# Category-conditioned matmul and ternary FFN on one core: the second product of two steps back issued ahead of the transposes of one step back

## The reference

```python
selected_W = W[cat_ids]
selected_b = b[cat_ids]
out = jnp.einsum('bsd,bdh->bsh', x, selected_W) + selected_b[:, None, :]
...
w_scale = jnp.mean(jnp.abs(weight)) + EPS
u = weight / w_scale
w_quant = u + jax.lax.stop_gradient(jnp.clip(jnp.round(u), -1.0, 1.0) - u)
a_scale = jnp.max(jnp.abs(x), axis=-1, keepdims=True) + EPS
z = jnp.clip(x / a_scale * 127.0, -128.0, 127.0)
a_quant = z + jax.lax.stop_gradient(jnp.round(z) - z)
y = jnp.einsum('bsi,oi->bso', a_quant, w_quant)
y = y * (w_scale * a_scale / 127.0)
...
x = x + _L0_ffn_ref(_L0_cond_ref(x, itok_B_0_63, L0_cond_W, L0_cond_b), L0_ffn_weight)
```

## Time and profile before

| | before |
|---|---|
| median of 3 runs | 546.17 us (544.36 to 547.55) |
| the profiled execution's own time | 543.38 us |
| its span, first to last instruction | 541.5 us |
| TensorE busy with matmuls | 512.7 us, 95% |
| VectorE, ScalarE, GpSimd busy | 392.5, 343.7, 281.2 us |
| TensorE clock granted, mean | 0.998 of 2.4 GHz |
| HBM traffic | 172.6 MB, 319 GB/s over the span |

### The profile page before, as it was taken

One profiled execution on the slowest core, in us unless ns is written; L12 is line 12 of the kernel. 1 busy time (PEld: TensorE's weight loads), 2 busy tenths in 40 slices (PEclk: granted clock), 3 DMA queues, 4 the chain that ended last, 5 costly groups with the idle time before them and its releaser, 6 DMA issues.

```text
span 541.5 us, 13855 instructions
## 1 busy us (share of the span) xinstructions
PE 512.7 (95%) x2584; PEld 355.8 (66%) x2585; DVE 392.5 (72%) x652; ACT 343.7 (63%) x502; POOL 281.2 (52%) x396
## 2 busy tenths in 40 slices
PE   4799999999999999999999998999989999999996
PEld 1576667666776666677676665667657677777774
DVE  3787765879667968966866858776797868758763
ACT  3577565765676567666756666766766666666753
POOL 3695455444556364555554463555446455565540
PEclk9999999999999999999999999999999999999999
DMA  5899879998899999979989889987999999899963
GB/s 170 276 404 351 291 258 310 382 364 274 324 364 343 367 333 392 356 243 372 350 291 294 325 322 398 365 288 271 407 332 363 329 363 342 273 310 333 323 194 117
DMA packets 71728, 172.76 MB, mean 319 GB/s; under 512 B 8096, under 2 KB 8224, under 8 KB 64800
## 3 DMA queue, kind: packets, MB, share of 16 engines
q1 hardware_dynamic: 71712, 172.59, 90.0%
HBM read 139.00 MB, written 33.55 MB: 319 GB/s over the span
## 4 chain that ended last, share of the span: by engine, by line
PE 35%; DVE 6%; issue 5%; DVEq 2%; ACT 2%; DMA 2%; ACTq 0%; SPq 0%; POOL 0%; POOLq 0%
PE ps_cond L619 9%; PE ps_cond L621 8%; PE ps_cond L620 8%; PE ps_y L587 8%; DVE sb_w_lo L486 3%; PE ps_aT L597 2%; DVE sb_absmax L527 2%; DMA sb_bias<-cond_b 2%; DVEq L165 1%; ACT sb_a_rounded L406 1%; ACT sb_w_hi L355 1%; DVE sb_a_step L530 0%; ACTq L165 0%; DVE sb_x_rows L520 0%; DVEq L486 0%
## 5 line engine op out<-in xcount | busy, mean ns | idle before, releaser
L619 PE MATMUL ps_cond<-sb_w_hi,sb_xT_hi 128*128 x512 | 220.7, 431 | 6.7 <-issue 3.2
L621 PE MATMUL ps_cond<-sb_w_hi,sb_xT_lo 128*128 x512 | 200.3, 391 | 0.0
L620 PE MATMUL ps_cond<-sb_w_lo,sb_xT_hi 128*128 x512 | 199.4, 389 | 0.0
L486 DVE TENSOR_TENSOR sb_w_lo<-sb_w_raw,sb_w_hi x106 | 162.1, 1567 | 20.2 <-issue 16.8
L317 POOL TENSOR_TENSOR sb_xT_lo<-sb_xT_raw,sb_xT_hi 128x512 fp32r<-128x512 f32 x128 | 166.4, 1300 | 10.9
L527 DVE TENSOR_REDUCE sb_absmax<-ps_cond 128x1 f32<-128x512 f32 x128 | 87.7, 686 | 100.6 <-PE ps_cond L621 89.1
L406 ACT ACTIVATE sb_a_rounded<-ps_cond,sb_rounder,sb_a_inv 128x512 f32<-128x512 f32 x128 | 99.5, 777 | 94.9 <-DVE sb_a_inv L533 94.5
L334 POOL TENSOR_SCALAR sb_y_scale<-sb_absmax,sb_w_step 128x1 f32<-128x1 f32 x128 | 41.0, 320 | 224.6 <-DVE sb_absmax L527 224.3
L587 PE MATMUL ps_y<-sb_ffnT,sb_aT 128*128 128x512 bf16 x512 | 131.2, 379 | 1.6 <-DVE sb_ffnT L512 0.9
L619 PEld LDWEIGHTS ps_cond<-sb_w_hi,sb_xT_hi 128*128 128x128 f32 x512 | 96.2, 188 | 51.7 <-issue 27.2
L396 ACT ACTIVATE sb_aT<-ps_aT 128x512 bf16<-128x512 int16 x128 | 75.4, 589 | 67.5 <-PE ps_aT L597 62.8
(11 more groups left out here) (69 smaller groups left out, 36.2 us busy)
## 6 DMA issues: line engine op xcount, KB each, us to landing
sb_w_raw<-cond_w SPq DMA_DIRECT2D x53, 1024.0 KB, 6.6
sb_xT_raw<-x_t SPq DMA_DIRECT2D x128, 256.0 KB, 5.1
sb_x_rows<-x SPq DMA_DIRECT2D x128, 256.0 KB, 5.2
out<-sb_x_rows SPq DMA_DIRECT2D x128, 256.0 KB, 4.9
sb_bias<-cond_b SPq DMA_DIRECT2D x54, 256.0 KB, 7.9
sb_ffn_raw<-ffn_t SPq DMA_DIRECT2D x1, 1024.0 KB, 6.9
sb_w_raw<-cond_w SPq DMA_DIRECT2D x4, 256.0 KB, 6.7
sb_cat_row_i<-itok SPq DMA_DIRECT2D x1, 64.0 KB, 3.5
```

Source lines behind the costliest of these rows:

```text
L486: dve.tensor_tensor(w_lo[:, bass.ds(at, PIECE)], w_raw[:, bass.ds(at, PIECE)], w_hi[:, bass.ds(at, PIECE)].bitcast(F32), ALU.subtract).the ...
L619: pe.matmul(ps_cond, x_hi_k, w_hi_k, start=False, stop=False, skip_group_check=True)
L620: pe.matmul(ps_cond, x_hi_k, w_lo_k, start=False, stop=False, skip_group_check=True)
L621: last_mm = pe.matmul(ps_cond, x_lo_k, w_hi_k, start=False, stop=(k == KD - 1), skip_group_check=True)
```

## The change

In TensorE's `body` the call of `second_product` for step r-2 now stands ahead of the call of `a_transpose` for step r-1. Nothing else is edited: the same instructions with the same waits are issued, in another order. The last step's extra calls stay where they are.

```diff
                 last_mm.then_inc(cond_mm_done, 1)
+                if not first or u >= Y_BEHIND:
+                    second_product(r - Y_BEHIND, (u - Y_BEHIND) % U, first)
                 if not first or u >= 1:
                     a_transpose(r - 1, (u - 1) % U, first)
-                if not first or u >= Y_BEHIND:
-                    second_product(r - Y_BEHIND, (u - Y_BEHIND) % U, first)
                 if last and u == U - 1:
```

## The result

The changed kernel takes 548.9 us as the median of 14 runs (547.26 to 551.08); the kernel before, run beside it, 546.15 us (14 runs, 543.98 to 547.79). The ratio is 1.0054, 95% interval 1.0036 to 1.0073. So the change costs 2.75 us, where 1.1 us less was forecast. The time lies at the upper end of the range of 541.5 to 549.5, just over the 2.7 us beyond which a slower kernel had been given 14%.

The account below looks back on a forecast made before the run. TensorE was taken to bound the kernel, losing 26.1 us in few late steps. Terms -2.3 + 0.4 + 0.24 + 0.6 = -1.1 us put the median at 546.2 - 1.1 = 545.1 us, range 541.5 to 549.5.

Parts of the forecast that it names:

- the later of C + 1.1 and A + chain: Start of TensorE's next step in a late step; 1.1 us is transposes plus second product, chain the sequencer's work behind A.
- C: Time in a step when TensorE is free, its last first-product matmul being done; 127.55 in step 27 before.
- A: Time when a_rounded, the rounding that the transposes wait for, ends; 128.60 in step 27 before.
- The gain in late groups, -2.3: Late steps joined where VectorE never waited: 19 groups, 17 saving 0.13 us each at the chain's front, plus 0.1.
- the bounds set (12 and 25): Sign of error: more than 25 or fewer than 12 late groups would mean VectorE's lag was changed by something left out.
- Slow reads, +0.4: The longest table read, 2149 ns in an on-time step, would start 0.4 us later; bounds 0 and 0.8.
- The end, +0.6: At the program's end the transposes of step 127 follow the second product of step 126, delaying all behind by 0.6 us.
- The start, +0.24: Transposes formerly done while the first second product waited for the ternary weight now follow it: 0.24 us more.
- ScalarE later by up to 0.5, hidden with 1 us to spare: Later transposes delay ScalarE's PSUM move, so a_rounded comes up to 0.5 us later in on-time steps, at no cost.
- rival 3: ScalarE becomes the late one: the later move delays rounding 0.5 us in late groups; +8.2 us, 554.4; chance 10%.
- Rival 1: The sequencer runs past the transposes' wait, so late groups lose up to 1.1 us less; -14.0, 532.2 us; chance 8%.
- Rival 2: Nothing saved at the front of the chain in late steps, only costs remain: +1.2, 547.4 us; chance 22%.

Follow-up runs that it names:

- the split order: Three of the second product's four matmuls ahead of the transposes, the fourth behind them, against the kernel before: 545.25 us, ratio 0.9969.
- the narrow last piece in the old order: Kernel before, no transposes moved, last second-product matmul of each step cut into 384 and 128 columns, narrow piece last: 548.59 us, ratio 1.0031.
- The two kernels without the split: Old and changed order, VectorE's split of the weights' low part left out from the second group of steps on: 523.5 and 529.34 us.
- both kernels with the bias three ahead: Three-plus-one second-product order and changed order, table read before the transposes' wait, bias written three steps ahead instead of two: 536.41 and 542.0 us.
- the split order with the early read and the bias two ahead: Three second-product matmuls, transposes, fourth matmul, with the next step's table read before the transposes' wait, against the kernel before: 540.69 us, ratio 0.9899.

## Why the prediction was wrong

- **The step that failed** is the sentence on the later of C + 1.1 and A + chain, "the first is the same sum in either order". It is not. In the old order the last thing ahead of the next first product is a matmul of 0.216 us, under which a float32 weight load disappears; in the new one it is a transpose of 0.056 us, and 0.055 us of the load shows. That is 6.5 us in 119 steps, and with the 19 ns inside the first product 8.7. TensorE's own part of the steps that are on time was costed at nothing, without comparing what stands at their end. Both numbers were there in the trace of before, a load of 0.19 us and transposes four to 0.24 us. Two experiments show the cause from either side: the split order (3.847 again) and the narrow last piece in the old order (3.893).
- **The gain in late groups, -2.3**, was right in its mechanism and mis-sized: the losses fell by 6.2 us. The chain fell by 0.13 us as forecast (the read 0.16 us behind A instead of 0.29; 1.48 to 1.51 us to L620). Much of the rest is a consequence of the failed step: a slower TensorE lets VectorE fall behind less, A - C of step 27 going from 1.05 to 0.82. The two kernels without the split put some 3 us (5.8 - 2.75, give or take some 2.5) on VectorE's lag; how the remainder divides is open. Late groups, joined where VectorE never waited for TensorE in between, went from 27 to 18 (from 22 to 12 if the wait right ahead of a late step is left out). The prediction's 19 are too few by either count: inside its groups 20 to 23, 46 to 51, 58 to 61 and 76 to 83 VectorE did wait. The count of after lies inside the bounds set (12 and 25) though the lag was changed: the test was too wide.
- **Slow reads, +0.4**, can't be checked singly: the longest is 2.03 us in the changed kernel, in step 58. What the reads in late steps took above 0.54 us, no more than each step's loss, sums to 5.8 us before and 5.1 after, so no such cost shows in the two traces. **The end, +0.6**: measured +0.63. **The start, +0.24**: the step with the first second product, step 2, became 0.20 us longer, close to the forecast. The whole start is 1.27 longer in the two profiled executions, of which 0.71 lies ahead of anything that the change touches and 0.29 is four steps at +0.073.
- **ScalarE later by up to 0.5, hidden with 1 us to spare**: right in on-time steps, where a_rounded ends 1.35 us ahead of C (before 1.70), and not quite right behind a high split. There the rounding starts right behind a move, in 8 late steps of either trace, but in the new order steps 9, 90 and 98 are among them, which were on time before. They lose 0.12, 1.10 and 0.31 us, step 90 mostly by a read of 1.62 us. That is rival 3's mechanism at 1.5 us or less, not at its price of 7.
- **Rival 1** (the sequencer runs past the wait) falls: in both orders no read of a late step started before A. The Trainium skill ("Perfetto Trace Analysis", section "Tensor Engine Instruction (MATMUL, LD_WEIGHTS)") would have it otherwise, and this case's traces disagree: 0.29 us behind A before, 0.16 after. **Rival 2** came nearest to the measured 548.9, with 547.4, by the wrong reason: the saving at the front of the chain is there.

## What to carry to other kernels

When matmuls are reordered, look at the pair that meets at each new junction: behind a short matmul the float32 weight load stuck out here, in every step, and not only in those that the change is meant for. A rearrangement that moves work ahead of a wait should leave one long matmul behind it. And when a wait is taken out of a chain, list what else ends near it: here the bias write alone would have held the next step until 1.16 us behind A, 0.3 us less than the read did, and in the split order taking the read away gave 4.6 us and then the bias 4.3 more.

## What the runs showed of the hardware that was not expected

- A float32 128x128 weight load takes 0.11 us from its start to the start of its matmul (recorded length 0.19), and hides behind a 512-column matmul of 0.216 us, but not behind 0.056 us.
- A read of the table by a sequencer takes longer the more values it asks for. On TensorE it is 0.54 us for two and 0.31 for one behind another read, on ScalarE 0.49 and 0.29, on SyncE 0.92 for seven (medians; single reads are slower, up to 2.7 us).
- The first product itself was 0.019 us longer in the changed order (2.308 against 2.289 us) and 0.012 shorter behind a narrow matmul of the second product (2.277). No experiment here says why.
- In both kernels with the bias three ahead, TensorE ran one first product at half speed, between 112 and 118 us. The table by stretch for the split one (length, busy us of PE, PEld, DVE, ACT, POOL with counts, granted clock, DMA share, GB/s):

```profile
105.00:110.00 5.00, 4.59 (x23) 2.99 (x23) 4.69 (x7) 1.68 (x4) 1.90 (x3) 1.00 0.92 301
110.00:112.50 2.50, 1.12 (x7) 0.76 (x8) 1.96 (x5) 2.19 (x5) 2.07 (x4) 0.97 1.05 395
112.50:116.00 3.50, 3.50 (x10) 2.69 (x10) 0.00 (x0) 2.54 (x4) 1.53 (x2) 0.54 1.00 368
```

The granted clock is 0.54 over 3.5 us, that is the level of 1.2 GHz, and matmuls stand 0.42 us apart instead of 0.23. Just before it TensorE was busy 1.12 of 2.50 us, waiting for a late rounding in step 23 and then for the table's read, which at the loop's jump stands behind it. It cost 1.6 us in the one execution and 1.4 in the other. No other profiled execution has such a first product behind step 8; the split order with the early read and the bias two ahead lost 2.08 us in the same step 23 and kept its clock. So the medians of these two kernels may hold a cost of that kind, and a version that waits less at that place would gain a little more; that was not tried.
